# Three slots for the gathered rows of a graph-attention edge loop, with the space taken from table and product buffers

## The reference, cut to what matters

```python
h = (x @ W.T).reshape(n, H, D)
h_src, h_dst = h[src], h[dst]
alpha = einsum('ehd,hd->eh', h_src, a_src) + einsum('ehd,hd->eh', h_dst, a_dst)
enc = relu(edge_attr @ edge_W.T + edge_b).reshape(-1, H, D)
alpha = leaky_relu(alpha + sum(enc * h_dst, axis=-1))
attn = softmax of alpha over the edges of each dst
out = segment_sum(h_src * attn[..., None], dst)
```

## Time and profile before

| | |
|---|---|
| median of three runs | 3758.8 us (3739.26 to 3773.95) |
| the profiled execution, its own time | 3765.38 us |
| its span, first to last instruction | 3763.1 us |
| granted TensorE clock, mean over the span | 0.777 |
| edge loop, first to last `raw` | 226.8 to 3177.0 us of the span |

### The profile page before, as it was taken

The page is one execution under the profiler, slowest core; times in us unless marked ns, Lnnn a source line. Parts: engine busy times, 40 slices in busy tenths (PEclk is TensorE's granted clock), DMA queues, the critical chain, the costliest instruction groups (busy, mean ns, idle before and its releaser), DMA issues. The chain is left out here.

```text
span 3763.1 us, 44207 instructions
## 1 busy us (share of the span) xinstructions
PE 2507.5 (67%) x8886; PEld 1669.8 (44%) x8886; DVE 2302.4 (61%) x3591; ACT 966.1 (26%) x3189; POOL 1905.5 (51%) x2039
## 2 busy tenths in 40 slices
PE   2547766666667676776766767666766665238998
PEld 1424444444444443444443444444444443017887
DVE  7846767666656676776666766666665655271223
ACT  3522222222222222222222222222222221042332
POOL 3655655555555555565555655555555553517000
PEclk9867778777777877777777777777787877558999
DMA  8244444445444444455444544444444896200000
GB/s 272 100 116 136 133 133 129 133 124 147 128 127 123 136 125 123 129 138 143 132 127 123 136 131 126 130 124 135 132 131 129 121 119 94 74 14 26 20 20 29
DMA packets 323290, 439.11 MB, mean 117 GB/s; under 512 B 115532, under 2 KB 258558, under 8 KB 322930
## 3 DMA queue, kind: packets, MB, share of 16 engines
q0 software_dynamic: 90000, 262.14, 28.5%
q1 hardware_dynamic: 232338, 175.80, 16.2%
q10 hardware_dynamic: 848, 0.26, 0.0%
HBM read 351.33 MB, written 86.62 MB: 116 GB/s over the span
## 5 line engine op out<-in xcount | busy, mean ns | idle before, releaser
L996 POOL DMA_INDIRECT src_in<-t_node_rows,rec_in x1760 | 1681.8, 956 | 1328.8 <-DVE weighted L1250 690.6
L1059 PE MATMUL p_sum<-weighted,hot 128*128 128x264 f32 x3520 | 1189.0, 497 | 80.0 <-DVE weighted L1250 41.9
L1059 PEld LDWEIGHTS p_sum<-weighted,hot 128*128 128x128 f32 x3520 | 865.1, 251 | 372.5 <-issue 115.1
L1200 DVE SCALAR_TENSOR_TENSOR prod<-p_enc,near 128x512 f32<-128x512 f32 x880 | 565.1, 684 | 685.4 <-ACT near L1122 408.1
L1250 DVE TENSOR_TENSOR weighted<-src_in,p_turn 128x1024 f32<-128x1024 f32 x440 | 534.7, 1216 | 295.4 <-issue 143.7
L1024 PE MATMUL p_pick<-ident,hot 128*128 128x128 f32 x440 | 166.5, 378 | 822.5 <-ACT hot L1106 576.7
L1204 DVE TENSOR_REDUCE dots<-prod 128x32 f32<-128x1024 f32 x440 | 536.9, 1220 | 15.2
L1024 PEld LDWEIGHTS p_pick<-ident,hot 128*128 128x128 f32 x440 | 67.9, 154 | 991.6 <-ACT hot L1106 556.5
L1038 PE MATMUL p_pick<-win,hotT 128*128 128x272 f32 x880 | 415.3, 562 | 68.2 <-issue 23.0
L1106 ACT ACTIVATE hot<-apart 128x128 f32<-128x128 f32 x440 | 136.0, 309 | 1144.6 <-remote 497.7
L1122 ACT COPY near<-p_pick 128x272 f32<-128x272 f32 x440 | 169.9, 386 | 977.6 <-remote 409.1
(11 more groups left out here) (334 smaller groups left out, 1630.3 us busy)
## 6 DMA issues: line engine op xcount, KB each, us to landing
win<-t_node_rows SPq DMA_DIRECT2D x440, 136.0 KB
t_block_sums<-sums SPq DMA_DIRECT2D x110, 528.0 KB
src_in<-t_node_rows,rec_in POOLq DMA_INDIRECT x1760
attrT<-t_block_attr SPq DMA_DIRECT2D x330, 36.0 KB
flags_in<-t_block_flags SPq DMA_DIRECT2D x440, 4.0 KB
t_node_rows<-out_rows SPq DMA_DIRECT2D x49, 136.0 KB, 1.7
x<-in_x SPq DMA_DIRECT2D x4, 1536.0 KB, 27.2
out_x<-x SPq DMA_DIRECT2D x48, 128.0 KB
```

Of the source, the lines that this page charges most:

```text
L996: pool.indirect_dma_start(src[:, q.par, b, k, :], None, scr["rows"], bass.IndirectOffsetOnAxis(ap=rec_i[:, q.par, b, k:k + 1], axis=0)).th ...
L1059: last = nc.tensor.matmul(p_sum[b % 2][:, 0:ROW], hot[:, q.par, b, :], weighted[:, b, k, :], start=(k == 0), stop=(k == W - 1))
L1200: nc.vector.scalar_tensor_tensor(prod[:, b % 2, 2 * half:2 * half + 2, :], p_enc[(PAIRS * b + half) % len(p_enc)][:, :, :], 0.0, near[:, q ...
```

## The change

- `src` gets `LAPS` = 3 slots in place of 2. A step has a second position, `q.slot` and `q.lap`, beside the parity; the gathers of block b of step q now wait for `weighted` of step q-3. The semaphores `s_src` go by slot.
- `prod` has one buffer in place of two, so `front` of DVE waits for the `dots` of the block before.
- The scratch of `expand` shares space: `turned` and `moved` with the row table `ro` and its small buffers, `new` with `near`, and the three bf16 parts of the attributes take turns in one buffer a third as large. The parts are made after steps 17, 19 and 21 of a group in place of 17 and 18, each stored by a DMA of its own; DVE waits for the earlier stores where it writes over them.
- SP's loop of 32 steps is written out, 96 steps in its program in place of the loop's 32; POOL's loop has six steps in place of two, with eight written out ahead of it in place of two.

```diff
-STORED_AT, LOADED_AT = 22, P // Q - RING - 2
+ROWS_AT, PARTS_AT, LOADED_AT = 2 * WAY_BITS, [2 * WAY_BITS + 1 + 2 * i for i in range(3)], P // Q - RING - 2
+STORED = 16 * 5

-        src = m.sb("src_in", [P, RING, Q, W, TABROW])
+        src = m.sb("src_in", [P, LAPS, Q, W, TABROW])
-        prod = m.sb("prod", [P, 2, W, D])
+        prod = m.sb("prod", [P, W, D])
-        parts = m.sb("l_parts", [P, KA, SLOTS], BF16)
+        attr_part = m.sb("l_parts", [P, EF, SLOTS], BF16)
+        space = m.sb("l_words", [P, 2 * SLOTS])
+        turned, moved = space[:, 0:SLOTS].bitcast(I32), space[:, SLOTS:].bitcast(I32)
+        n_ro = P * (W + 1)
+        ro = space[:, 0:n_ro].rearrange("p (r w) -> p r w", w=W + 1)

             def load_rows(q):
                 if q.since(RING):
-                    before = q.prev().prev()
+                    before = straight(q.s - RING)
                     for b in range(Q):
-                        sp.wait_ge(s_src[q.par][b], 16 * W * q.turn)
+                        sp.wait_ge(s_src[before.slot][b], 16 * W * (before.lap + 1))

-            with nc.sync.Fori(0, GROUPS - 1) as i:
+            for i in range(GROUPS - 1):
                 for u in range(turn):
                     if u == LOADED_AT:
-                        sp.wait_ge(s["table_stored"], i * 48 + 49)
-                    body(grouped(i, u))
-                    if u == STORED_AT:
-                        store_group(i, P)
+                        sp.wait_ge(s["table_stored"], STORED * (i + 1))
+                    body(straight(RING + i * turn + u))
+                    if u == ROWS_AT + 1:
+                        store_group(i)
+                    for part in range(3):
+                        if u == PARTS_AT[part] + 1:
+                            store_group(i, part)

             def gather(q):
-                    if q.since(RING):
-                        pool.wait_ge(s["weighted"], Q * q.prev().prev().s + b + 1)
+                    if q.since(LAPS):
+                        pool.wait_ge(s["weighted"], Q * (q.s - LAPS) + b + 1)
-                        pool.indirect_dma_start(src[:, q.par, b, k, :], None, scr["rows"],
+                        pool.indirect_dma_start(src[:, q.slot, b, k, :], None, scr["rows"],
-            loop(nc.gpsimd, gather, last)
+            both = RING * LAPS
+            whole, rest = (STEPS - LAPS) // both, (STEPS - LAPS) % both
+            for k in range(LAPS + rest):
+                gather(straight(k))
+            with nc.gpsimd.Fori(0, whole) as i:
+                for u in range(first, first + both):
+                    gather(Step(i * both + u).of(i * LAPS + u // RING, u % RING).lapped(i * RING + u // LAPS, u % LAPS))

             def front(q, b):
                 dve.wait_ge(s["near"], n + 1)
+                if n:
+                    dve.wait_ge(s["dots"], n)

+                    if i:
+                        dve.wait_ge(s["table_stored"], STORED * i)
+                    if i or part:
+                        dve.wait_ge(s["table_stored"], STORED * i + (16 * (part + 2) if part else 0))
```

More of the change, by code:

```diff
@@ L121, in store_table, with store_attrs @@
     nc.sync.dma_start(scr["block_flags"][block, :], flags[0:n, :]).then_inc(stored, 16)
-def store_attrs(nc, scr, b0, n, parts, stored):
+def store_attrs(nc, scr, b0, n, parts, stored, part=None):
     block = bass.ds(b0, n) if not isinstance(b0, int) else slice(b0, b0 + n)
-    nc.sync.dma_start(scr["block_attr"].rearrange("c (b s) -> b c s", s=SLOTS)[block, :, :], parts[0:n, :, :]).then_inc(stored, 16)
+    to = scr["block_attr"] if part is None else scr["block_attr"][EF * part:EF * (part + 1), :]
+    nc.sync.dma_start(to.rearrange("c (b s) -> b c s", s=SLOTS)[block, :, :], parts[0:n, :, :]).then_inc(stored, 16)
 class Chain:
@@ L760 @@
 RING = 2
+LAPS = 3
 class Step:
@@ L771, in of, with lapped @@
         self.turn = i
+        return self
+    def lapped(self, lap, slot):
+        self.lap = lap
+        self.slot = slot
         return self
@@ L827, in edge_loop @@
         last_new = m.sb("last_new", [P, GROUPS])
[L828 to L830 removed]
         head_flags = m.sb("l_flags", [P, P])
[L832 to L833 removed]
+        attr_part = m.sb("l_parts", [P, EF, SLOTS], BF16)
[3 more added lines that the diff above has]
+        ro = space[:, 0:n_ro].rearrange("p (r w) -> p r w", w=W + 1)
+        small = {n: space[:, n_ro + i * P:n_ro + (i + 1) * P] for i, n in enumerate(("near", "ok", "place"))}
+        assert n_ro + 3 * P <= 2 * SLOTS
+        small["new"], small["near"] = small["near"], small["near"].bitcast(I32)
         last_of = m.sb("last_of", [ITILES - 1, 1])
@@ L849, in edge_loop @@
         s_win = [m.sem(f"s_win_loaded{i}") for i in range(RING)]
-        s_src = [[m.sem(f"s_gathered{i}{q}") for q in range(Q)] for i in range(RING)]
+        s_src = [[m.sem(f"s_gathered{i}{q}") for q in range(Q)] for i in range(LAPS)]
         s_stored = [m.sem(f"s_sums_stored{i}") for i in range(RING)]
@@ L1204, in front @@
                 nc.vector.tensor_reduce(dots[:, q.par, b, :, :].rearrange("p k h -> p (k h)"),
-                                        prod[:, b % 2, :, :].rearrange("p k (h d) -> p (k h) d", h=H), AX.X, ALU.add).then_inc(s["dots"], 1)
+                                        prod[:, :, :].rearrange("p k (h d) -> p (k h) d", h=H), AX.X, ALU.add).then_inc(s["dots"], 1)
             def scores(q):
                 for b in range(Q):
-                    dve.wait_ge(s_src[q.par][b], 16 * W * (q.turn + 1))
+                    dve.wait_ge(s_src[q.slot][b], 16 * W * (q.lap + 1))
                 dve.wait_ge(s["dots"], Q * (q.s + 1))
                 flat = lambda v: v.rearrange("p q k h -> p (q k) h")
-                nc.vector.tensor_tensor(flat(raw[:, :, :, :]), flat(dots[:, q.par, :, :, :]), flat(src[:, q.par, :, :, D:ROW]), ALU.add).then_inc(s["raw"], 1)
+                nc.vector.tensor_tensor(flat(raw[:, :, :, :]), flat(dots[:, q.par, :, :, :]), flat(src[:, q.slot, :, :, D:ROW]), ALU.add).then_inc(s["raw"], 1)
                 dve.wait_ge(s["raw"], q.s + 1)
@@ L1249, in weigh @@
                 heads = lambda v: v.rearrange("p k (h d) -> p k h d", h=H)
-                nc.vector.tensor_tensor(heads(weighted[:, b, :, 0:D]), heads(src[:, q.par, b, :, 0:D]),
+                nc.vector.tensor_tensor(heads(weighted[:, b, :, 0:D]), heads(src[:, q.slot, b, :, 0:D]),
                                         spread(p_weight[:, b, :, :], HD), ALU.mult).then_inc(s["weighted"], 1)
             def body(q, ahead=True):
-                n, before = q.next(), q.prev()
+                n, before = straight(q.s + 1), straight(q.s - 1) if q.s else None
                 scores(q)
```

44 lines of the change are left out of this document (19 added, 25 removed).

## The result

The changed kernel takes 3972.9 us (median of 4 runs, 3964.5 to 3974.3), the kernel before 3749.0 us beside it (4 runs, 3738.1 to 3774.0). The ratio is 1.056, with an interval of 1.052 to 1.060: 5.6% slower. The forecast was 3732 us with a range up to 3788, so the result lies outside the range and on the other side.

The account below looks back on a forecast made before the run. It took the edge loop as bound by a chain across engines, its end perhaps by transfers. Gains of 4.7 us in the main part and 22 in the end part, with 0.4 back, gave 3732 us, range 3692 to 3788.

Parts of the forecast that it names:

- the slower rival: Around SP's loads: steadier gathers overlap more transfers, so PE's results come later; 15 to 56 us slower; chance 0.18.
- What bounds the kernel.: Edge loop: no compute engine full, a chain across engines binds; PE's late results are a large part of 27.1 us.
- I leave it alone: Main part of the edge loop: the mean step stays; a change over 0.3 us would prove the prediction wrong.
- The lead.: Step 52: time from its last gather's end to `raw` grows from 5.4 to 31 us, worth 4.7 us in the main part.
- 22 us in the end part: Loop's end: gain from earlier gathers, taken between 18.0 us if no window comes earlier and a bound of 27.1.
- the rival of the windows: End part: SP's windows queue behind earlier gathers, `raw`'s waits become waits of picks; only 4.7 us gained, 3754 us; chance 0.20.
- The paying edits at nothing.: One `prod` buffer, attribute parts, `expand` waits, SP's and POOL's rewritten loops: no cost but 0.4 us for markers.
- the 22 that the text kept for the upper end: DVE's 440 more `prod` waits: 22 us if the sequencer needed 0.05 us for each on the path.
- The Trainium skill's rule: PE and ACT never wait on anyone, so the rival of later PE results could not be; expected time stays.

Follow-up runs that it names:

- the short pause with two slots: The kernel before, with its two slots, plus one waited memset of 256 columns on POOL ahead of each block of four gathers: 3507.6 us, ratio 0.938.
- the short pause in both kernels: One waited memset of 256 columns on POOL ahead of each four gathers, added to the changed kernel (3504.2 us, 0.927) and the kernel before (3507.6 us, 0.938).
- The release half a step on: The changed kernel with each block's gathers waiting for a `weighted` two blocks later, so half the lead is kept: 3844.7 us, ratio 1.018.

## Why the prediction was wrong

The step that failed is the sentence with which it turned down the slower rival: "gathers keep their rate and their phase within the step, since `weighted` of step q-3 comes at the same place in a step as that of q-2". The same text let the gathers start when the table has landed, 25 us earlier, while `weighted` of step q-3 comes a whole step of 27.1 us earlier. So it is the table that sets the start, and the blocks behind it find their slots free; the rival itself had said that they would "run more steadily". In the run, POOL waited 485.7 us for the table, 76 times, and the gathers lost many of the stops that `weighted` had put between their blocks (1.0 a step in place of 1.7). 71% of them stood in runs of more than eight, in place of 29%. Such runs hold PE's results back, shown by the pauses: with them the remote waits of the loop go from 12.7 us a step to none. With this the prediction's premise falls too that POOL's 621.9 us of waiting were "no loss: nobody stands behind POOL but `raw`": the stops also kept PE's results from coming still later.

Point by point:
- *What bounds the kernel.* Right in kind: a chain across engines with PE's late results in it. But the late results were laid to the loop's transfers, taken as a given and only moved by some per cent. They stand for 9.7 us of waiting in a step of 27.07, of which the kernel before loses at least 27.07 - 24.88 = 2.2 us, as the short pause with two slots shows ((2921.2 - 208.9) / 109 = 24.88 us a step).
- *"I leave it alone"*, the mean step of the main part. It moved by 1.83 us, where the prediction's own sign of being wrong was 0.3 us.
- *The lead.* Right in kind: 40.0 us for step 52 where 31 were worked out, the table landed about 3 us after its issue, and `raw` waits for no gather any more. It was worth nothing, since what `raw` no longer waits for came back as waits of `hot`, `near` and `weighted`.
- *22 us in the end part.* They didn't come. `raw` waits there no longer, nor does any pick wait for `win`, so the rival of the windows didn't come either; but in the stretch from 3140 to 3380 us ACT's and DVE's remote waits are 56.9 + 44.9 + 32.4 + 4.3 = 138.5 us, against 28.2 + 23.4 = 51.6 before. By the starts of `raw` the last 8 steps take (3375.6 - 3129.6) / 8 = 30.75 us each, in place of (3177.0 - 2941.4) / 8 = 29.45.
- *The paying edits at nothing.* Nearly right. With the slot's timing undone they leave 0.6% (0.3 to 0.9%), 23 us, near the 22 that the text kept for the upper end. Which of them it is was not tried, nor does any run show the 0.05 us for each wait that the 22 came from: it was an assumption, and the likeness of the numbers is luck. With the short pause in both kernels nothing of the loss is seen (0.927 and 0.938).
- *The slower rival.* Right in kind and place, too small by four times: it had 15 to 56 us, the result is 224. It was sized as a tenth more of 833.9 us; over the same number of steps ACT's and DVE's remote waits rose by 30%, and the chance of 0.18 rested on the argument that failed. The cause in it was also wrong: not more transfers at once, as the run with 32-byte rows shows, but gathers issued more densely.
- *The Trainium skill's rule* ("SBUF — State Buffer", section "Who interferes with whom"), that PE and ACT never wait on anyone, is a statement on the ports of SBUF; read as widely as the prediction read it, it would have left no room for this result. These runs show a result of PE taken 9.3 us late beside gathers, and none late with a pause; the measurement decides. Whether SBUF is the place, no run here tells.

**What stays open.** The runs tell when PE's results are held back (gathers made closer than one in about 1.5 us, over more than four to six of them) and that the bytes are not the cause. They don't tell where inside the chip this happens, nor whether signals of DVE, ACT and POOL are held back in the same way. The 0.6% of the paying edits isn't divided. The release half a step on lies between the two others as its long runs do, but why its remote waits are the lowest of the three isn't seen.

## What to carry to other kernels

An earlier start of a transfer is not free when another engine has to make it: ask how densely that engine will then issue, and who stands still beside it. Where PE's consumers show long "remote" waits and POOL issues indirect DMAs at the same time, try a waited pause of about a us between every few of them, before any work on buffers; here one memset and one wait a block made either kernel 6 to 7% faster than the kernel before, and the third slot gave nothing that is clear of noise. A wait that looks like a loss (POOL's 621.9 us for `weighted`) can be what keeps another engine from being later still.

## What was unexpected of the hardware

- Results of PE reach the waiting engine late while POOL makes indirect gathers back to back: 9.7 us of such waits in a step of 27.07 before, 12.7 in one of 28.89 after, 0.1 when 4 gathers of 1.255 us are followed by 1.30 us without one, and none with 1.76 us.
- The late result is mostly taken in a stop of POOL, later the more gathers stood in the run: 1.4 us behind four, 1.7 behind eight, 2.5 behind twelve (medians, kernel before).
- The lateness doesn't come from the bytes of the gathers: at 47 GB/s and a DMA share of 0.21 the step was 28.78 us, at 122 GB/s and 0.45 it was 28.89.
- A waited memset of 128x8 costs POOL 0.12 us of work and 0.97 us until the next gather starts; behind a memset of 128x256 that POOL does not wait for, the next gather starts after 0.16 us.
- With results on time, a step of sixteen gathers is bound by POOL making them, 24.1 of 24.78 us, though POOL stands at six tenths on the page of that run.
